# Moving one head's long filter from between the first pair's solve levels to between the second pair's, with the attended values of two heads in another bank

## The reference, cut to what matters

```python
v_direct = silu(short_conv(h @ Wv.T)); q, k likewise        # 4 heads of 128
u = T @ (v * beta)          # T = inverse of a unit triangular 64x64 matrix per sequence and head
delta_out = attn @ u        # attn = causal (q k^T)
local_s, local_m, local_l = fir(v_direct, 3 taps), fir(.., 15 taps), fir(.., 63 taps)
o = p0*local_s + p1*local_m + p2*local_l + p3*delta_out + p4*v_direct     # p: gate probabilities
x = x + rmsnorm(o) @ Wo.T
x = x + ffn(layernorm(x))   # shared experts first, then routed ones
```

## Time and profile before

| | |
|---|---|
| median of 3 runs | 468.88 us (468.72 to 470.0) |
| the profiled execution | 472.15 us, of which span 470.3 us |
| busy share of the span | PE 92%, PEld 61%, DVE 66%, ACT 37%, POOL 16% |
| mean granted TensorE clock | 0.969 of full |
| chain that ended last | PE 74%, DVE 11%, issue 4%, POOL 3%, SP's queue 3% |
| same chain by line | experts' matmuls L916 32%, levels L731 7%, long filters L653 4% |
| first pair's levels from the third step on, and second pair's | 159 to 198 us, 198 to 238 us |

### The profile page before, as it was taken

The page is one execution under the profiler, slowest core; times in us unless marked ns, Lnnn a source line. Parts: engine busy times, 40 slices in busy tenths (PEclk is TensorE's granted clock), DMA queues, the critical chain, the costliest instruction groups (busy, mean ns, idle before and its releaser), DMA issues.

```text
span 470.3 us, 8091 instructions
## 1 busy us (share of the span) xinstructions
PE 434.7 (92%) x3140; PEld 285.8 (61%) x3140; DVE 308.4 (66%) x572; ACT 175.2 (37%) x235; POOL 74.9 (16%) x78
## 2 busy tenths in 40 slices
PE   4999999999989799999999799967988999999985
PEld 2943347643555556778663578843436788888862
DVE  5551236697887978976479645304117999999964
ACT  1102111669542111113240631103008687887630
POOL 2000000000206500157420000660000000000071
PEclk9999999999999799999599999996999999999999
DMA  8999959665024410190002000676009999999544
GB/s 319 431 428 426 430 208 309 196 175 155 2 91 97 144 32 3 60 388 5 1 0 91 1 1 1 222 174 209 0 14 419 367 384 397 388 405 408 207 127 145
DMA packets 17937, 92.41 MB, mean 196 GB/s; under 512 B 3424, under 2 KB 5104, under 8 KB 10736
## 3 DMA queue, kind: packets, MB, share of 16 engines
q1 hardware_dynamic: 14880, 78.82, 44.6%
q10 hardware_dynamic: 1488, 8.93, 5.4%
q0 software_dynamic: 1536, 4.20, 2.8%
HBM read 82.25 MB, written 12.08 MB: 201 GB/s over the span
## 4 chain that ended last, share of the span: by engine, by line
PE 74%; DVE 11%; issue 4%; POOL 3%; SPq 3%; DMA 2%; another core or an unknown queue 2%; ACT 1%; DVEq 0%; ACTq 0%; POOLq 0%
PE bank L916 32%; PE bank L731 7%; PE bank L653 4%; PE bank L679 3%; PE bank L516 3%; PE bank L562 3%; PE bank L540 3%; PE bank L583 3%; POOL ring L431 2%; SPq L329 2%; DVE part L1469 2%; PE bank L704 2%; DMA cols<-cols_in 2%; PE bank L893 2%
## 5 line engine op out<-in xcount | busy, mean ns | idle before, releaser
L1469 DVE SCALAR_TENSOR_TENSOR part<-ring,cols,part 128x504 f32<-128x504 f32 (+13 forms) x64 | 42.4, 722 | 0.1
L731 PEld LDWEIGHTS bank<-ring 64*64 64x64 f32 x960 | 34.4, 144 | 12.3 <-issue 8.3
L731 PE MATMUL bank<-ring 64*64 64x64 f32 (+1 forms) x960 | 38.9, 235 | 3.0 <-POOL ring L431 2.6
L679 PE MATMUL bank<-xnT,ring 128*128 128x512 f32 (+1 forms) x96 | 37.7, 544 | 0.7 <-ACT xnT L1055 0.7
L653 PE MATMUL bank<-early,ring 128*32 128x512 f32 (+15 forms) x512 | 34.4, 409 | 0.0
L422 POOL TENSOR_TENSOR small<-small 128x1 f32<-128x1 f32 (+2 forms) x12 | 12.0, 1003 | 134.0 <-DVE small L1346 73.8
L1469 DVE SCALAR_TENSOR_TENSOR ring<-bank,cols,ring 128x504 f32<-128x504 f32 (+2 forms) x36 | 26.3, 733 | 5.1 <-ACT ring L1103 4.1
L679 PEld LDWEIGHTS bank<-xnT,ring 128*128 128x128 f32 x96 | 17.7, 190 | 17.1 <-issue 14.5
L1237 ACT ACTIVATE rows<-bank 128x512 f32<-128x512 f32 x19 | 11.3, 597 | 44.6 <-PE bank L916 26.3
L431 POOL TENSOR_TENSOR ring<-ring,consts 128x256 f32<-128x256 f32 x20 | 16.3, 839 | 51.3 <-DVE ring L1601 36.5
L916 PE MATMUL bank<-early,hTa 128*128 128x512 f32 x32 | 17.1, 683 | 7.4 <-DVE hTb L1739 7.4
(11 more groups left out here) (256 smaller groups left out, 914.7 us busy)
## 6 DMA issues: line engine op xcount, KB each, us to landing
early<-wffn_in SPq DMA_DIRECT2D x21, 1024.0 KB, 7.7
ring<-ctxT_in SPq DMA_DIRECT2D x4, 2048.0 KB, 25.9
ring<-ctx_in SPq DMA_DIRECT2D x4, 2048.0 KB, 30.3
raw1b<-wffn_in SPq DMA_DIRECT2D x6, 1024.0 KB, 9.7
raw3b<-wffn_in SPq DMA_DIRECT2D x6, 1024.0 KB, 6.9
raw2b<-wffn_in SPq DMA_DIRECT2D x6, 1024.0 KB, 8.3
ring<-firw_in SPq DMA_DIRECT2D x4, 1024.0 KB, 5.0
xs<-zeros_in ACTq DMA_DIRECT2D x1, 3840.0 KB, 14.0
```

Of the source, the lines that this page charges most:

```text
L679: last = pe.matmul(bank[QB[g % 3]][:, ts], wqkv[:, j, c, h * P:(h + 1) * P], xnT[:, c, ts], start=(c == 0), stop=(c == DC - 1))
L731: last = pe.matmul(dst[s, d], left[s, L * t:L * (t + 1)], right(s, t), start=True, stop=True)
L1469: return dve.scalar_tensor_tensor(out=d, in0=s, scalar=w, in1=d, op0=ALU.mult, op1=ALU.add)
```

## The change

In the first pair only head 2's filter is left, 2 rounds in each of steps 2 to 9, where 4 rounds of head 2's and then 4 of head 3's stood. Head 3's 16 rounds go into steps 0 to 5 of the second pair, as 3, 3, 2, 3, 2, 3. ACT's copies of heads 2 and 3 move with them. The attended values of heads 0 and 1 go to bank 6 instead of 7, one step later (3 and 5), DVE's additions follow (n = 4 and 6), and the square sums of both heads stand in step 8.

```diff
@@ between_first
-                if 2 <= step < 6:
-                    fir_rounds(2, 4 * (step - 2), 4 * (step - 1))
-                if step >= 6:
-                    fir_rounds(3, 4 * (step - 6), 4 * (step - 5))
+                if step >= 2:
+                    fir_rounds(2, 2 * (step - 2), 2 * (step - 1))
@@ between_second
-                if step == 2:
-                    pe.wait_ge(S["fir_kept"], H)
-                    attended(0, 7)
-                if step == 4:
+                if step == 3:
+                    pe.wait_ge(S["u_ready"], 2)
+                    attended(0, 6)
+                if step == 5:
                     pe.wait_ge(S["o_ready"], 1)
-                    attended(1, 7)
-                if step == 6:
+                    attended(1, 6)
+                if step == 8:
+                    pe.wait_ge(S["o_ready"], 2)
                     square_sums(0, 6)
-                if step == 8:
                     square_sums(1, 6)
+                if step < 6:
+                    fir_rounds(3, (0, 3, 6, 8, 11, 13)[step], (3, 6, 8, 11, 13, FW)[step])
                 if step < 8:
                     weights_spread(step)
                 else:
-                    pe.wait_ge(S["o_ready"], 2)
+                    pe.wait_ge(S["fir_kept"], H)
                     keep_warm(bank[7][:, :], 1)
@@ ACT, levels of both pairs
-                    if pair == 0 and l == NLV // 2:
-                        keep_fir(2)
                     if pair == 1 and l == 3:
+                        keep_fir(3)
                         squares(1)
                 if pair == 0:
-                    keep_fir(3)
+                    keep_fir(2)
@@ DVE, updates of the second pair
-                if n in (3, 5):
-                    add_attended(n // 2 - 1, 7)
+                if n in (4, 6):
+                    add_attended(n // 2 - 2, 6)
```

## The result

The changed kernel takes 486.54 us (median of 4 runs, 485.59 to 490.58) beside 469.44 us (468.72 to 471.02, 4 runs) for the kernel before: the ratio is 1.0376, 95% interval 1.0311 to 1.0441. It is slower by 17.1 us. I had said 477.3 us, range 473.0 to 482.5: right in sign, wrong in size by a factor of two. Repeated on another chip the ratio was 1.0367 (1.0306 to 1.0427).

What follows compares the result with a forecast made beforehand. PE was taken to bound both pairs, DVE close behind in the first. Terms -4.0 + 7.9 + 5.0 - 0.5 = +8.4 us, added to the median of 468.88, gave 477.3 us, range 473.0 to 482.5.

Steps and rivals of the forecast that it cites:

- What bounds: Both pairs: PE bounds them, with DVE close behind in the first pair and far behind in the second.
- Term 1: Second pair, steps 0 to 5: head 3's 16 filter rounds add 7.9 us to PE's stream.
- Term 2: First pair: less filter work on PE gives back 4.0 us, including one clock loss of 1.9 us.
- DVE's floor: End of first pair: with DVE's idle pieces gone, the second pair's first Z can't start before 191.8 us.
- Term 3: Second pair, after step 5: ACT waits for the first weight load and stalls PE, +5.0 us.
- late load: Rival at ACT's weight wait: load takes 10.1 us, stall 10.3, total +13.7, 482.6 us; chance 0.06.
- Term 4: Tail, step 6's Z to out projection: an earlier clock drop behind the stall changes it by -0.5 us.
- Costed at nothing: Moved attended values, filter copies, bank 7 and SP's later loads: taken to cost no time.
- the filter's work keeps the clock up: Rival in second pair and tail: no drop follows the stall, tail gives 3.4 us, +5.5, 474.4 us; chance 0.10.
- A first pair that gives nothing back: Rival in first pair: low clock keeps the second pair's start near 197.7 us, +12.4, 481.3 us; chance 0.09.
- a faster kernel: Rival over both pairs: full clock and no ACT wait give -1.4 us, 467.5 us; chance 0.05.
- the views that I named: Profile after: first Z at 191.8 to 195 us, PE gap near 187, 7.9 us more filter, 5 us stall, half clock.

Runs made afterwards that it cites:

- e1: Changed kernel with ACT's rounding of the first raw weight moved to the second pair's last level; 464.74 us beside 462.78, ratio 1.0046.
- e2: Kernel before with only the change's attended values, additions and square sums, filters all in the first pair; 458.43 us beside 460.90, ratio 0.9951.
- e5: Changed kernel with ACT's fourth-filter copy ahead of its load wait and 9 unread matmuls on PE during the stall; 473.17 us beside 460.90.
- e4: Kernel before with SP's five weight loads also waiting for the second pair's step 5 Z; 471.05 us beside 462.78, ratio 1.0182.
- e8: Kernel before with only head 0's square sums moved from step 6 to step 8 of the second pair; 468.03 us beside 470.92, ratio 0.9925.
- e9: e2 without the unread matmul in step 8 of the second pair; 467.20 us beside 470.92 for the kernel before, ratio 0.9905.
- after_again: Changed kernel unedited, timed and profiled again beside the kernel before on one chip; 477.30 us beside 460.90, ratio 1.0367.
- e10: e5 with 6 unread matmuls on PE during the stall in place of 9; 479.72 us beside 470.92 for the kernel before, ratio 1.0165.

## Why the prediction was right in kind and wrong in size

- *What bounds.* Right. PE pays for moved work in the second pair in full, DVE caps what the first pair gives back.
- *Term 1, +7.9.* Measured 8.2 us (e1 against e2).
- *Term 2, -4.0.* Profile against profile it was -4.1, and its parts hold. DVE's floor was 191.8 - 159.1 = 32.7 us behind R: in the one profile with PE's gap but no drop behind it (e5), update n = 8 ends 32.5 us behind R and the first Z comes at 33.0. The gap was 2.43 us (2.3 forecast), and with the drop the stretch is 34.5 us in three profiles, so the drop cost 1.5 us (1.9 forecast). But the baseline was bad. The 38.6 us of the first profile hold the low stretch at 158 us. I took the gap of 2.60 us as enough for such a drop; every version has this gap, and the clock fell in it or within 1 us behind it in 6 of the 13 profiles. At full clock the first pair takes 36.3 us (e2, e4, e8, e9). Against that the gain is 1.8 us.
- *Term 3, +5.0.* Right: stall 4.88 us, landing 4.76 us (4.8 taken), rounding 1.91 us. The late load (L = 10.1) is refuted: the first of the five loads landed in 4.76 us although SP issued the other four within 2.5 us behind it.
- *Term 4, -0.5.* This is the step that failed. Profile against profile it was +3.8; against the tail at full clock it is 23.85 (the mean of two profiles) - 15.5 = +8.3. Both profiles of the kernel before have the low tail, 10.4 us of it at half clock, but some executions can't have had all of it: three of the 13 timed beside after_again have mean clocks of 0.990 and 0.994, by my estimate at most 9.2 us at half clock in the whole span (2 x 0.010 x 459). I had priced the drop behind the stall like the one at 158 us, 5.9 us of half clock, and let the clock recover after it. That drop had a dense filter piece behind it. The tail has levels, spreads and square sums behind the stall, and the clock stayed low for 20 us, until the second of its matmuls that nobody reads (246.04 for 2.00 us; the window at 247 us has 0.55, the next 1.00). In the kernel before, after_again and e4, too, it came back at this matmul. That the small work behind the stall keeps the clock down fits these rows but isn't shown by itself: no run changed what follows the stall. My upper end, all of the tail at half clock, was +4.7, and I gave it little chance; also my full-clock tail of 16.6 us, worked out with the factor 1.49 of the filter, should have been 15.5, since the tail's small matmuls slow by 1.97/1.15 = 1.7.
- *Costed at nothing.* The attended part with the square sums was worth -4.5 us in the tail when no stall follows. In timed runs it is worth 2.5 to 2.9 us (e2, e8). The stall hid that in the changed kernel.

*The sum.* From the kernel before at its best in all three stretches, 36.3 + 20.6 + 15.5, to the changed one, 34.5 + 33.6 + 23.85, it is -1.8 + 8.2 + 4.9 + 8.3 = +19.6 us; from its first profile -4.1 + 8.2 + 4.9 + 3.8 = +12.8. The timed runs, +17.1 and +16.4, lie between, as the kernel before meets its low stretches in some executions and not in others. I took one execution's low stretches for the kernel's. In terms of the forecast, the 8.4 us became 17.1 like this: 4.4 us more in the three stretches, nearly all of it term 4; 1.7 us ahead of R; and 2.6 us because I carried the 3.3 us between the first profile and the median over to the changed kernel, whose profile lies at its median (486.58 and 486.54). What remains open is the 1.7 us ahead of R in the first pair of profiles, and why the clock falls at 158 to 164 us in some executions only.

The rivals: that the filter's work keeps the clock up isn't borne out. Without the stall the tail does run at full clock (e1), but with all filter work in the first pair it does so too (e2, e8), and behind the idle PE it doesn't. A first pair that gives nothing back (4.1 us in the profile), a late load, and a faster kernel did not come. Of the views that I named, all showed what I said but two: the first Z at 195.3 us stands 1.7 us later than the terms say, by the shift ahead of R, and the half clock behind the stall lasted more than three times as long as priced. The Trainium skill's fit of "DMA: Bandwidth & Descriptors", "Anatomy of one DMA", is by its heading one for DMAs that GpSimd issues; the 4.4 us that I worked out from it are 0.4 us under the 4.76 us of SP's load here.

## What to carry to other kernels

When work is moved past a point that releases DMA loads, look for the in-order engine that touches the first of these loads and for what is queued behind it: here one rounding on ACT, 1.9 us of work, turned into a 4.9 us stall of PE and 8 us of lost clock. Don't price a stall of PE by its length alone: a gap of 2.6 us ahead of filter rounds cost 1.1 to 2.3 us of clock where the clock fell at all (37.4 and 38.6 against 36.3 us), one of 4.9 us ahead of small matmuls 8. Length and following work differ together in these two; which of them counts wasn't separated. And before taking a stretch of one profile as baseline, set its mean clock beside that of other executions; a stretch at 0.92 isn't the kernel's, it is that execution's.

## What the runs showed of the hardware that I had not expected

- With PE busy without a gap, the clock can still fall: before, at 223 us. Moving 0.98 us of matmuls with one output column out of step 6 kept it at 1.00 through the tail (e8); the kernel was 0.3 to 1.2% faster.
- One idle gap of 4.9 to 5.2 us was followed by 20 us at 1.2 GHz in three profiles (changed, after_again, e4), and the gap filled with 5.4 us of matmuls that nobody reads by none in that tail (e10).
- The same gap of 2.4 us in the first pair was followed by 3.4 us of half clock in the changed kernel and by none in e5, which is 33.0 against 34.5 us for the stretch. A drop followed this gap in six of the seven profiles that have it, and the 2.60 us gap at R in 6 of 13, so a forecast has to carry both cases.
